# Attention on one Trainium2 core: the softmax sums inverted over 128 partitions by 16 columns, with a round trip through DRAM

## The reference

```python
q, k, v = (heads(x @ W + b) for W, b in ...)            # layer 0; layer 1 has no bias
attn = q @ k.T / sqrt(64) + rel_bias_h + rel_bias_w     # layer 0: all 1024 keys
attn = softmax(attn)                                    # layer 1: 7x7 neighbours only
out = (attn @ v) @ Wp + bp
```

## Time and profile before

| | |
|---|---|
| median of 3 runs | 3626.62 us (3626.27 to 3631.67) |
| the profiled execution's own time | 3628.03 us |
| its span, first to last instruction | 3626.2 us |
| TensorE busy, mean granted clock | 3339.9 us (92%), 0.976 |
| VectorE busy | 1635.4 us (45%) |
| ScalarE busy | 1197.9 us (33%) |
| GpSimd busy | 1084.4 us (30%) |
| moved by DMA | 210.92 MB, mean 58 GB/s |

### The profile page before, as it was taken

One profiled execution on the slowest core, in us unless ns is written; L12 is line 12 of the kernel. 1 busy time (PEld: TensorE's weight loads), 2 busy tenths in 40 slices (PEclk: granted clock), 3 DMA queues, 4 the chain that ended last, 5 costly groups with the idle time before them and its releaser, 6 DMA issues.

```text
span 3626.2 us, 48881 instructions
## 1 busy us (share of the span) xinstructions
PE 3339.9 (92%) x21248; PEld 2394.7 (66%) x21248; DVE 1635.4 (45%) x1477; ACT 1197.9 (33%) x1301; POOL 1084.4 (30%) x612
## 2 busy tenths in 40 slices
PE   7988898998998888999899888999989988899998
PEld 5864557776785445777678544577767854457776
DVE  4346534435434653433553455344354345633443
ACT  3334432133324443213332444321323244432142
POOL 0036660024003666003300466500330056650042
PEclk9999999998999999999999999999999999999999
DMA  3110012104311001211431100221043111021113
GB/s 136 66 35 18 15 37 103 35 30 134 125 56 27 18 18 35 102 36 33 130 125 56 29 18 16 60 78 43 27 138 116 55 33 18 12 78 67 36 30 102
DMA packets 158707, 210.92 MB, mean 58 GB/s; under 512 B 110496, under 2 KB 110752, under 8 KB 158496
## 3 DMA queue, kind: packets, MB, share of 16 engines
q1 hardware_dynamic: 158496, 207.81, 18.5%
HBM read 132.26 MB, written 50.33 MB: 50 GB/s over the span
## 4 chain that ended last, share of the span: by engine, by line
PE 65%; DVE 15%; issue 12%; ACT 4%; SPq 2%; DMA 1%; POOL 1%; ACTq 0%; DVEq 0%; POOLq 0%
PE score L855 14%; PE score L856 12%; PE score L857 12%; PE head_out L977 7%; DVE max_part L661 6%; PE mx L912 6%; PE score L947 4%; PE mx L915 3%; DVE recip L690 2%; SPq L328 2%; PE mx L930 2%; DVE o_raw L695 2%; ACT b_lo_raw L464 1%; DVE b_lo L681 1%; PE score L954 1%
## 5 line engine op out<-in xcount | busy, mean ns | idle before, releaser
L422 POOL TENSOR_TENSOR acc<-acc,prob 128x1024 f32<-128x1024 f32 x288 | 721.1, 2528 | 245.3 <-ACT prob L560 245.3
L560 ACT ACTIVATE prob<-score 128x1024 f32<-128x1024 f32 (+3 forms) x576 | 514.7, 907 | 645.9 <-PE score L960 547.9
L661 DVE TENSOR_REDUCE max_part<-mx 128x2 f32<-128x1024 f32 x384 | 467.7, 1218 | 422.3 <-PE mx L915 422.3
L977 PE MATMUL head_out<-prob,v 128*64 128x512 f32 (+4 forms) x2496 | 490.7, 518 | 0.0
L855 PE MATMUL score<-a_hi,w_hi 128*128 128x512 f32 x1152 | 463.8, 403 | 29.0 <-DVE a_lo L651 26.4
L856 PE MATMUL score<-a_lo,w_hi 128*128 128x512 f32 x1152 | 452.9, 393 | 0.0
L857 PE MATMUL score<-a_hi,w_lo 128*128 128x512 f32 x1152 | 451.7, 392 | 0.0
L422 POOL TENSOR_TENSOR acc<-prob 128x1024 f32<-128x1024 f32 x48 | 113.5, 2387 | 996.9 <-ACT prob L560 811.0
L912 PE MATMUL mx<-k_hi,q_hi 64*128 64x512 f32 (+2 forms) x1152 | 265.8, 452 | 124.8 <-DVE max_part L661 109.7
L855 PE MATMUL score<-w_hi,a_hi 128*128 128x256 f32 x1152 | 346.4, 301 | 0.0
L856 PE MATMUL score<-w_lo,a_hi 128*128 128x256 f32 x1152 | 325.6, 283 | 0.0
(11 more groups left out here) (98 smaller groups left out, 5351.9 us busy)
## 6 DMA issues: line engine op xcount, KB each, us to landing
raw<-weights SPq DMA_DIRECT2D x96, 768.0 KB, 4.3
g_mem<-g SPq DMA_DIRECT2D x24, 1024.0 KB, 4.0
recip<-recip SPq DMA_DIRECT2D x384, 64.0 KB, 2.0
xin<-x_t SPq DMA_DIRECT2D x24, 512.0 KB, 6.2
xr<-x_t SPq DMA_DIRECT2D x24, 512.0 KB, 5.0
x_mem<-xr SPq DMA_DIRECT2D x24, 512.0 KB, 3.8
xr<-x_mem SPq DMA_DIRECT2D x24, 512.0 KB, 6.4
y_t<-xr SPq DMA_DIRECT2D x24, 512.0 KB, 4.1
```

The source lines that it names most:

```text
L422: nc.gpsimd.tensor_tensor(acc[:, :, a:b], with_, now, ALU.add).then_inc(added, 1)
L560: nc.scalar.activation(prob[:, ug % P_SLOTS, :, 0:b - a], score[:, u % 2, :, 0:b - a], ACT.Exp, scale=SCALE).then_inc(prob_ok, 1)
L661: nc.vector.reduce_max(max_part[:, t, part, :], mx[:, :, 0:b - a], AX.X).then_inc(max_ok, 1)
L977: last = nc.tensor.matmul(head_out[rows_of(h), half, x - half * HALF:y - half * HALF], v[:, t, p * 128 + 64 * h:p * 128 + 64 * h + 64], pr ...
```

## The change

The four distinct rows of `sums4`, partitions 0, 32, 64 and 96, are sent by one DMA into `sums16`, 128 partitions by 16 columns. One reciprocal of 128x16 goes to `recip16`. A second DMA writes that to a DRAM tensor `r_mem` of 2 rows (the heads) by 1024 tokens. A third reads each of its rows 64 times into `recip[:, p, :]`. SyncE waits between them. `recip4` is gone, and `invert` is one instruction, which in layer 0 stands behind maximum 5.

```diff
+    sums16 = m.put("sums16", [128, 2 * TOKENS // 128])
+    recip16 = m.put("recip16", [128, 2 * TOKENS // 128])
...
             def spread(f, p):
-                sp.wait_ge(recip_ok, 2 * pair_no(f, p))
-                for n in range(4):
-                    for k in range(2):
-                        a = 64 * (n // 2) + 32 * k
-                        sp.dma_start(recip[a:a + 32, p, n % 2 * HALF:(n % 2 + 1) * HALF],
-                                     recip4[32 * n:32 * n + 32, :]).then_inc(recip_in, 16)
+                sp.wait_ge(sums_out, pair_no(f, p))
+                if pair_no(f, p) > 1:
+                    sp.wait_ge(recip_ok, pair_no(f, p) - 1)
+                sp.dma_start(sums16[:, :], sums4[0:128:32, :]).then_inc(sums_in, 16)
+                sp.wait_ge(recip_ok, pair_no(f, p))
+                if pair_no(f, p) > 1:
+                    sp.wait_ge(recip_in, 16 * (pair_no(f, p) - 1))
+                sp.dma_start(r_mem.rearrange("h (j c) -> (h j) c", c=16), recip16[:, :]).then_inc(recip_sent, 16)
+                sp.wait_ge(recip_sent, 16 * pair_no(f, p))
+                rows = bass.AP(r_mem.tensor, 0, [[TOKENS, 2], [0, 64], [1, TOKENS]])
+                sp.dma_start(recip[:, p, :], rows).then_inc(recip_in, 16)
...
             def sums_copy(f, p):
                 act.wait_ge(sum_mm, pair_no(f, p))
                 if pair_no(f, p) > 1:
-                    act.wait_ge(recip_ok, 2 * (pair_no(f, p) - 1))
+                    act.wait_ge(sums_in, 16 * (pair_no(f, p) - 1))
...
-            def invert(f, p, part):
-                if part == 0:
-                    dve.wait_ge(sums_out, pair_no(f, p))
-                    if pair_no(f, p) > 1:
-                        dve.wait_ge(recip_in, 128 * (pair_no(f, p) - 1))
-                cols = slice(part * CHUNK, (part + 1) * CHUNK)
-                nc.vector.reciprocal(recip4[:, cols], sums4[:, cols]).then_inc(recip_ok, 1)
+            def invert(f, p):
+                dve.wait_ge(sums_in, 16 * pair_no(f, p))
+                if pair_no(f, p) > 1:
+                    dve.wait_ge(recip_sent, 16 * (pair_no(f, p) - 1))
+                nc.vector.reciprocal(recip16[:, :], sums16[:, :]).then_inc(recip_ok, 1)
...
-                        if p and k in (3, 4):
-                            invert(f, p - 1, k - 3)
+                        if p and k == 5:
+                            invert(f, p - 1)
```

More of the change, by code:

```diff
@@ L166, in build @@
 def build(nc, x_in, w_in, bqk_in, bv_in, bp_in, rel_in, onehot_in, mask_in, group_src, ident_in,
-          g_mem, x1_mem, y_out):
+          g_mem, x1_mem, r_mem, y_out):
     blocks = group_blocks()
@@ L181, in build @@
     sums4 = m.put("sums4", [128, HALF], at=one + 44 * KB)
-    recip4 = m.put("recip4", [128, HALF], at=one + 46 * KB)
     two = m.at
@@ L248, in build @@
     g_sent, bias_in, recip_in = sems("g_sent", G_SLOTS), sems("bias_in", SETS), sem("recip_in")
+    sums_in, recip_sent = sem("sums_in"), sem("recip_sent")
     bn_ok, mv_ok, gsum_ok, gmv_ok, shift_ok, shift2_ok = (sem(n) for n in (
@@ L378, in _ @@
                         if i == CT - 1:
-                            sp.wait_ge(recip_in, 128 * pair_no(f, last))
+                            sp.wait_ge(recip_in, 16 * pair_no(f, last))
                         sp.dma_start(xin[:, i, :], x_in[image + 1, :, i, :]).then_inc(xin_in[i], 16)
@@ L682, in bias_lo @@
                                         ALU.subtract).then_inc(b_lo_ok, 1)
-            def invert(f, p, part):
-                if part == 0:
-                    dve.wait_ge(sums_out, pair_no(f, p))
-                    if pair_no(f, p) > 1:
-                        dve.wait_ge(recip_in, 128 * (pair_no(f, p) - 1))
-                cols = slice(part * CHUNK, (part + 1) * CHUNK)
-                nc.vector.reciprocal(recip4[:, cols], sums4[:, cols]).then_inc(recip_ok, 1)
+            def invert(f, p):
[3 more added lines that the diff above has]
+                nc.vector.reciprocal(recip16[:, :], sums16[:, :]).then_inc(recip_ok, 1)
             def normalise(f, p):
-                dve.wait_ge(recip_in, 128 * pair_no(f, p))
+                dve.wait_ge(recip_in, 16 * pair_no(f, p))
                 dve.wait_ge(out_copied, pair_no(f, p))
@@ L782, in _ @@
                         if p:
-                            invert(f, p - 1, 0)
-                            invert(f, p - 1, 1)
+                            invert(f, p - 1)
                         if p >= 2:
@@ L805, in _ @@
                     out_lo(f, last - 1)
-                invert(f, last, 0)
-                invert(f, last, 1)
+                invert(f, last)
                 normalise(f, last)
@@ L1168 @@
     x1_mem = nc.dram_tensor("x1_mem", (128, CT, TOKENS), F32, kind="Internal").ap()
+    r_mem = nc.dram_tensor("r_mem", (2, TOKENS), F32, kind="Internal").ap()
     y = nc.dram_tensor("y_t", (IMAGES, 128, CT, TOKENS), F32, kind="ExternalOutput").ap()
-    build(nc, *args, g_mem, x1_mem, y)
+    build(nc, *args, g_mem, x1_mem, r_mem, y)
     r = run_bass_kernel_spmd(nc, [arrays], core_ids=[0])
```

## The result

The changed kernel takes 3888.76 us (median, 3875.97 to 3896.54) against 3629.14 us before, a ratio of 1.0712 with a 95% interval of 1.0681 to 1.0743. It is 260 us slower. The forecast of 3960 us had the sign and the mechanism; the loss it forecast, 334 us on the profiled execution, was 28% too large.

What follows compares the result with a forecast made beforehand. The chain was taken to lie 65% on TensorE and 15% on VectorE. Layer 0's middle pairs 162, its last pair 52 and layer 1 120 us sum to 334 on 3628.0, rounded to 3960 us; range 3860 to 4065.

Steps and rivals of the forecast that it cites:

- Rival 1: Last transfer spread over 16 engines, landing in 3.9 us: 3613 us, faster by 0.4%; chance 0.09.
- A: Pairs 1 to 4 of layer 0, 16 in all: normalisation 8.05 us later, plus 2 us of clock; 162 us.
- B: Last pair of layer 0: 4 x (1.2 inside the pair + 9.0 at its end + 2.8 of half clock) = 52 us.
- C: Layer 1: pairs slowed to a 16.7 us loop, last normalisation at 910.6 against 880.62; 4 x 30.0 = 120 us.
- Rivals 2 and 3: Last transfer on one engine: 4370 us, chance 0.03; on 4 engines: 3690 us, with 8 about no change, chance 0.05.
- 40 us for each microsecond: Whole kernel: each further microsecond of the last transfer's landing costs some 40 us over layer 0 and layer 1.
- the half clock: In layer 0's pairs 1 to 4, idle TensorE runs 5.6 us at half speed, some 2 us not hidden by VectorE.
- its longer part: From the last pair of layer 0 to layer 1's first sums: forecast +47 us.
- The loop: Layer 1: normalise(p-2), invert(p-1) and the queue take 16.7 us a pair, more than the 12.77 of the rest.
- nothing would be left over of VectorE's saving: Whole kernel: the 167 us VectorE saves lay in its idle time or are in the differences already counted.

Runs made afterwards that it cites:

- the first experiment: The changed kernel with its third transfer cut into two reads, one for each head, 64 rows each: 3596.80 us, ratio 0.9911 to the kernel before.

## Why the prediction was right, and where its sizes were off

**The third transfer** was taken at 12.1 us on two engines, and in pair 2 it landed 12.36 us behind the start of its issue, at 0.13 of the engines. With the rule of the Trainium skill ("DMA: Bandwidth & Descriptors", "Why a DMA increments its semaphore by 16 and not by 1") the trace agrees: 2 engines here (a share of 0.13), 4 for the source of four rows (0.26), 16 for the reads of 64 rows (1.01). Rival 1, sixteen engines, gave 3613 us; the first experiment made it true at 3596.8 us. Its terms were -2, +3 and -16 us for A, B and C; measured were -0.5, -1.1 and -31.2. It had no term for the clock that TensorE keeps at layer 1's end. Rivals 2 and 3 did not occur.

**Each issue was counted twice.** A landing in these profiles counts from the start of the issue. The 2.0 us of the 64 KB row so hold the 0.6 us of its issue, as the chain of the kernel before shows (the seventh of eight issues, then the eighth from its start to its landing, then the normalisation behind it):

```profile
816.55 0.59 SPq L328
817.18 1.99 DMA recip<-recip
819.20 0.04 DVE o_raw L695
```

The prediction added 0.6 us to it for the gather, the write and the read. For write and read that is 1.2 us too much in every pair, by the forecast's own 40 us for each microsecond some 50 us in all (an estimate), most of the 74 us by which the sum came out too high. Other errors, of both signs, make up the rest. The measured 3889 us lies near the lower end of the range, 3860.

**The sum at A failed in size**, 55 of the 74 us too much. Three terms. The write was priced at 2.6 us and took 1.41: 0.6 was the issue counted twice, 0.6 that the 64 KB row is too dear for 8 KB. The read, 0.6 + 12.1 = 12.7 us in the sum, took 12.36. Normalisation was 6.6 us later in pair 2 and 6.8 in the mean of the 16 pairs, not 8.05. "A wait of VectorE before L695 is paid by TensorE, 1:1" left out that the waiting changes the work behind it: GpSimd runs out of exponentials meanwhile, no add is running, and normalisation takes 1.23 us instead of 2.73. That returns 1.5 us in each of 16 pairs. And for the half clock 1.4 us a pair remain, not 2, as the rest of the 6.7 us a pair: 6.7 - (6.8 - 1.5). The clock term itself was not isolated by a run.

**B** came 9 us lower in its longer part: the last normalisation started 17.4 us behind its sums copy (580.59 against 563.20), not 19.2, 7 us in four images; 1.2 of the 1.8 us is the write again. Within the last pair it came 3 us lower, presumably since GpSimd's backlog hid the late exponentials nearly whole.

**C** was 111 us for 120, by two errors of opposite sign. The loop was 15.2 to 15.7 us and not 16.7, mostly the write again. At the end, the terms for the last two reads were too small: the sum had nothing for the residual, `group` and `xin` loads issued behind them. These loads fill the other engines, all engines slow down together (17.5 instead of 26 GB/s each, in the two stretches above), and the reads land 14.7 and 16.0 us behind the start of their issues.

**That nothing would be left over of VectorE's saving** was right for the change as made. It doesn't hold once the read is spread: the route with the small reciprocal is then worth 39 us against the best other one tried.

## What to carry to other kernels

Look at the outermost count of both sides of a DMA, not only at its bytes: a broadcast from two rows ran on two of sixteen engines, and the same broadcast written as two DMAs ran on all, which turned a kernel slower by 7% into one faster by 1%; a DMA share of 0.13, 2 of 16, over a long landing is the sign of it. Then look at how many SBUF partitions the engines read: sixteen on one partition made the slowest kernel of all, 15% slower than the kernel before. Before time is saved on an engine, ask what stands behind it in program order: moving three waiting operations by a few slots was worth 40 to 50 us, and taking the wide reciprocals off VectorE 30 to 40 us, and that only with the read spread.

## What the runs showed of the hardware that was not expected

- A DMA on two engines and later ones on the same queue delay each other. Loads of 512 KB issued behind it fill the other engines and stretch it from 12.4 to 16.0 us; their own landings go from 6.2 to 16.6 us (medians), and the first lands 1.2 us behind it. That fits loads whose share on the two engines waits until the read is done (8 packets at 0.16 us are 1.3 us); the profile doesn't name the engine of a packet, so this is argued.
- Sixteen engines reading one SBUF partition move 35 GB/s together, sixteen neighbouring partitions 114 GB/s; two engines reading two partitions 64 apart move 50 GB/s. One DRAM row read 64 times by sixteen engines shows no such limit (311 GB/s).
- An 8 KB write to DRAM completes 1.41 us behind the start of its issue, sooner than the 64 KB transfer between SBUF rows (2.0 us).
- The contention on VectorE is a wait and not a slower rate: normalisation takes 1.2 us beside an idle GpSimd, and otherwise ends 1.08 us behind the running add, up to 3.4 us in all, so its time moves with the schedule.
